# A transformer block with top-2 experts: inputs laid out transposed on the host, weight folds on TensorE, and another split of the batches over two groups

## The reference, cut to what matters

```python
Wm = W_attn + (lora_A @ lora_B).reshape(W_attn.shape)      # 384 x 128
xa = batchnorm(x @ Wm.T)            # mean and variance over all tokens
q, k, v = split(xa)
y = softmax(causal(q @ k.T / sqrt(128))) @ v
y = y @ W_proj.T @ (W_proj + lora_pA @ lora_pB).T
x = layernorm(x + y)
gates = top2(softmax((ln(x) * r_scale + r_bias) @ router_w.T + router_b))
h_e = gelu((ln(x) * scale_e + bias_e) @ w1[e].T + b1[e])    # 8 experts, 512 hidden
x = layernorm(x + sum_e gates_e * (h_e @ w2[e].T + b2[e]))
```

## Time and profile before

| what | us |
|---|---|
| median of three runs | 638.56 |
| the profiled execution, own time | 633.27 |
| its span, first to last instruction | 631.5 |
| start, until the first row maximum of the attention | 42.4 |
| attention, until the first tile's transpose | 185.5 |
| experts, 142 tiles | about 362 |
| tail after the last matmul | about 41 |

### The profile page before, as it was taken

One profiled execution on the slowest core, in us unless ns is written; L12 is line 12 of the kernel. 1 busy time (PEld: TensorE's weight loads), 2 busy tenths in 40 slices (PEclk: granted clock), 3 DMA queues, 4 the chain that ended last, 5 costly groups with the idle time before them and its releaser, 6 DMA issues.

```text
span 631.5 us, 15137 instructions
## 1 busy us (share of the span) xinstructions
PE 476.5 (75%) x3652; PEld 448.1 (71%) x3652; DVE 287.1 (45%) x1617; ACT 364.6 (58%) x934; POOL 301.9 (48%) x361
## 2 busy tenths in 40 slices
PE   7969566585756959777778887778899999999300
PEld 6868455575655859777767876777899999999300
DVE  0178454655545964222222221212333588783393
ACT  0338354553643866544454554445677788998483
POOL 4002655556552005445655444545344476675573
PEclk9979797897977979878889777788799999999755
DMA  9950111111112012222221221222122456543362
GB/s 227 358 147 14 44 44 40 35 40 44 39 44 62 2 32 69 59 60 78 74 66 56 57 56 54 58 61 60 53 65 80 139 155 168 168 121 115 91 195 72
DMA packets 66049, 53.70 MB, mean 85 GB/s; under 512 B 11986, under 2 KB 59218, under 8 KB 65970
## 3 DMA queue, kind: packets, MB, share of 16 engines
q1 hardware_dynamic: 53136, 33.27, 19.8%
q0 software_dynamic: 8640, 17.97, 8.7%
q10 hardware_dynamic: 4194, 1.53, 1.0%
HBM read 28.43 MB, written 24.31 MB: 84 GB/s over the span
## 4 chain that ended last, share of the span: by engine, by line
PE 64%; another core or an unknown queue 11%; issue 6%; ACT 6%; DVE 5%; DMA 5%; SPq 2%; ACTq 0%; POOL 0%; POOLq 0%; DVEq 0%
PE bank L803 24%; PE bank L813 22%; PE bank L796 3%; PE bank L705 3%; DMA ld_bc<-L_ffn_expert_ln_bias 2%; PE bank L691 2%; SPq L383 1%; PE bank L714 1%; PE bank L763 1%; PE bank L752 1%; DMA xT<-ybuf 1%; DMA x_all<-L_attn_x 1%; PE bank L765 1%; PE bank L764 1%
## 5 line engine op out<-in xcount | busy, mean ns | idle before, releaser
L549 POOL DMA_INDIRECT ybuf<-xT,yrow x142 | 137.3, 967 | 183.5 <-DVE yrow L1278 134.9
L803 PE MATMUL bank<-xT 128*128 128x128 f32 x1136 | 167.9, 296 | 34.3 <-issue 20.0
L803 PEld LDWEIGHTS bank<-xT 128*128 128x128 f32 x1136 | 152.3, 209 | 36.8 <-issue 21.6
L813 PE MATMUL bank<-w2T,xT 128*128 x1136 | 164.9, 292 | 13.1 <-ACT xT L948 11.5
L538 POOL DMA_INDIRECT queue<-x_all,pos_i x128 | 123.1, 962 | 94.6 <-DVE pos_i L1196 56.3
L813 PEld LDWEIGHTS bank<-w2T,xT 128*128 128x128 f32 x1136 | 150.7, 206 | 17.2 <-issue 16.7
L1268 DVE TENSOR_TENSOR xT<-bank,b_bc 128x128 f32<-128x128 f32 x142 | 41.4, 292 | 221.5 <-PE bank L813 120.4
L835 ACT ACTIVATE xT<-w1T,zero_col 128x512 f32 x142 | 102.3, 721 | 31.2 <-issue 24.0
L948 ACT ACTIVATE xT<-bank 128x512 f32<-128x512 f32 x142 | 82.7, 583 | 23.8 <-PE bank L803 21.0
L835 ACT ACTIVATE xT<-bank,one_col 128x128 f32<-128x128 f32 x142 | 51.6, 364 | 76.0 <-remote 35.7
L1275 DVE TENSOR_SCALAR xT<-xT 128x128 f32<-128x128 f32 x142 | 49.4, 348 | 2.4 <-issue 1.5
(11 more groups left out here) (220 smaller groups left out, 750.5 us busy)
## 6 DMA issues: line engine op xcount, KB each, us to landing
xT<-queue SPq DMA_DIRECT2D x142, 66.0 KB
xT<-ybuf SPq DMA_DIRECT2D x32, 256.0 KB
x_all<-L_attn_x SPq DMA_DIRECT2D x16, 256.0 KB, 6.2
w_rows<-L_ffn_w SPq DMA_DIRECT2D x16, 256.0 KB, 8.8
out<-x_all SPq DMA_DIRECT2D x32, 128.0 KB
ybuf<-xT,yrow POOLq DMA_INDIRECT x142
queue<-x_all,pos_i POOLq DMA_INDIRECT x128
queue<-pad_rows SPq DMA_DIRECT2D x2, 528.0 KB, 13.7
```

The lines of the kernel that those rows point to most:

```text
L549: pool.indirect_dma_start(out=ybuf, out_offset=bass.IndirectOffsetOnAxis(yrow[:, q:q + 1], 0), in_=ysb[:, q, :], in_offset=None).then_inc( ...
L803: last = mm(bank[2 + s][:, h * P:(h + 1) * P], w1c[:, (q - 1) % XR, h * P:(h + 1) * P], xgT[:, s, :], start=True, stop=True)
L813: last = mm(bank[4 + s][:, 0:P], hs[:, s, h, :], w2T[:, bass.ds(e, 1), h, :].rearrange("p a d -> p (a d)"), start=(h == 0), stop=(h == HC ...
```

## The change

The host now hands over x also transposed (`x_t`), w1 and w2 transposed, the small parameters packed in two arrays (`wide`, `low`) and b1 in three copies. Device code changes as follows.

- x chunks are loaded by SP (even) and ACT (odd); xT comes straight from `x_t` in eight loads of four batches. No transposes of x or of weights are left, nor their copies of x and w2.
- Two `fold_round`s in place of four. PE does seven matmuls on zeros before the first chunk.
- The scale, bias and b1 go into w1 on PE: per expert one float32 matmul with `fold_l[e]` (identity times scale, plus bias less scale over C) and one bfloat16 matmul that adds b1 in three parts. Three experts before the attention, five in steps 0 to 4, each with one copy by ACT. DVE's `fold_expert` is gone; it makes `dl`, `pick_b` and `b1s` in the start, ACT makes `fold_l`.
- DVE's second and third part of `split_constant` come after the row maxima of step 0; PE's `start_v(0)` waits for them (s_cv).
- NB0 is 18, so NTILE0 is 79 and group 1 has 63 tiles; COUNT0 is 21. BETWEEN is 5: 14 batches, before tiles 0, 5, ..., 65. LAG is 12, YR is 24; `yb` lies in the buffer of w1's rows. FIN stays at 18, so no batch is loaded ahead of `results_written(NTILE)`.
- In the tail a store is that of the batch five back.

```diff
-    NB0 = 20
+    NB0 = 18
-        XR, YR = 4, 16
+        XR, YR = 4, 24
-        LAG = 7
+        LAG = 12
-            BETWEEN = 6
+            BETWEEN = 5
@@ sync
-            for c in range(NCH):
+            def load_columns(c):
+                here = slice(c * XT_B * T, (c + 1) * XT_B * T)
+                sp.dma_start(xT[:, here], x_t[:, here]).then_inc(s_xt[c], 16)
+            for c in range(0, NCH, 2):
                 load_chunk(c)
+            load_columns(0)
             for e in range(E):
-                load_w1(e)
+                sp.dma_start(w1r[:, e], w1_t[:, e]).then_inc(s_w1[e], 16)
+                if e == E - 2:
+                    load_columns(1)
+            for c in range(2, NB // XT_B):
+                load_columns(c)
...
             for n in range(max(FIN, NB0), NB):
                 load_y(n)
-                store(stored)
-                stored += 1
+                if stored <= n - 5:
+                    store(stored)
+                    stored += 1
@@ tensor
+            def fold_w1(e):
+                pe.wait_ge(s_w1[e], 16)
+                if e == 0:
+                    pe.wait_ge(s_fl, 1)
+                    pe.wait_ge(s_b1s, 1)
+                wait(pe, s_wc, e if e > W1_FIRST else e - W1_FIRST + 1)
+                mm(fold_bank(e)[:], fold_l[:, e, :], w1r[:, e], start=True, stop=False)
+                mm(fold_bank(e)[:], pick_b[:, e, :], b1s[:], start=False, stop=True).then_inc(s_wt, 1)
...
-                if X_STEP <= k < W_STEP:
-                    transpose_chunk(EARLY_X + k - X_STEP)
-                elif W_STEP <= k < W_STEP + 2 * E:
-                    transpose_weights(k - W_STEP)
+                if k + W1_FIRST < E:
+                    fold_w1(k + W1_FIRST)
@@ scalar
+            act.dma_start(low_s[:], low).then_inc(s_small, 16)
+            act.dma_start(wide_s[:], wide).then_inc(s_small, 16)
+            act.dma_start(rb[:], r_b.unsqueeze(0)).then_inc(s_small, 16)
...
+            for c in range(1, NCH, 2):
+                act.dma_start(x_all[:, c * CH:(c + 1) * CH, DATA:DATA + P], x_chunks[c]).then_inc(s_x[c], 16)
+                if c == 3:
+                    act.dma_start(b1f[:], b1_rows).then_inc(s_b1f, 16)
...
+            for e in range(E):
+                last = act.activation(fold_l[:, e, :], ident[:], ACT.Identity, bias=dl[:, e:e + 1],
+                                      scale=lsT[:, e:e + 1])
@@ vector
-            v.wait_ge(s_ls, 48)
-            op(v.tensor_tensor(ld_bc[:], ld_bc[:], ls_bc[:], ALU.subtract))
-            op(v.tensor_scalar(b1c[:], b1c[:], 1.0 / C, None, ALU.mult))
...
-                if 0 <= k - FOLD_STEP < 3 * (E - 1):
-                    fold_expert(1 + (k - FOLD_STEP) // 3, (k - FOLD_STEP) % 3)
+                if known == 0:
+                    for n in range(1, 3):
+                        split_constant(n)
+                    v.sem_inc(s_cv, 1)
```

More of the change, by code:

```diff
@@ L222, in build, with fold_bank @@
         r_bias = sb("r_bias", [P, E])
[L225 to L247, removed]
+        w1r = sb("w1r", [P, E, H])
+        dl = sb("dl", [P, E])
+        fold_l = sb("fold_l", [P, E, P])
+        b1f = sb("b1f", [P, H])
+        b1p = sb("b1p", [P, H], BF16)
+        b1s = sb("b1s", [P, H], BF16)
+        own = sb("own", [P, E])
+        warm = sb("warm", [P, P])
+        pick_b = sb("pick_b", [P, E, P], BF16)
+        W1_FIRST = 3
+        def fold_bank(e):
+            return bank[(6, 4, 5)[e] if e < W1_FIRST else 6]
         s_w1 = [sem(f"s_w1_{e}") for e in range(E)]
-        s_w2, s_ls, s_w1p, s_wt, s_wc = [sem(n) for n in ("s_w2", "s_ls", "s_w1p", "s_wt", "s_wc")]
+        s_w2, s_wt, s_wc, s_dl, s_fl, s_b1s = [sem(n) for n in ("s_w2", "s_wt", "s_wc", "s_dl", "s_fl", "s_b1s")]
         U = 4
@@ L594, in _ @@
             mm, tr = pe.matmul, pe.transpose
-            pe.wait_ge(s_one, 1)
             gram = bank[7][:, 0:P + 1]
+            pe.wait_ge(s_warm, 1)
+            for n in range(N_WARM):
+                mm(bank[6][:, 0:P], warm[:], warm[:], start=True, stop=True)
             def fold_round(r):
@@ L654, in _ @@
             last.then_inc(s_gram, 1)
-            for c in range(2):
-                transpose_chunk(c)
             pe.wait_ge(s_cov, 1)
-            mm(bank[2][:, 3 * P + 2 * E:3 * P + 3 * E], wp2[:], wvvT[:, 0:E], start=True, stop=True)
             for g in range(3):
@@ L663, in _ @@
             last.then_inc(s_proj, 1)
-            for c in range(2, 9):
-                transpose_chunk(c)
+            mm(bank[2][:, 3 * P + 2 * E:3 * P + 3 * E], wp2[:], wvvT[:, 0:E], start=True, stop=True).then_inc(s_wr, 1)
+            for e in range(W1_FIRST):
+                fold_w1(e)
             pe.wait_ge(s_qk, 1)
@@ L868, in _, with copy_w1 @@
+            last.then_inc(s_fl, 1)
+            def copy_w1(e):
+                act.wait_ge(s_wt, e + 1)
+                cp(w1T[:, e, :], fold_bank(e)[:], bias=zero_col[:]).then_inc(s_wc, 1)
+            for e in range(W1_FIRST):
+                copy_w1(e)
             act.wait_ge(s_mt, 1)
@@ L1097, in _, with split_constant @@
             pg.settle()
-            for n in range(3):
+            def split_constant(n):
                 op(v.tensor_copy(cvp[:, n, :], cv[:]))
```

242 lines of the change are left out of this document (110 added, 132 removed).

## The result

The changed kernel takes **654.94 us** in the median of four runs (648.42 to 657.68), the kernel before beside it 638.72 (638.44 to 640.36): ratio 1.0258, 95% interval 1.0205 to 1.0310. It is slower by 16 us; 8 us faster was forecast, and 654.94 lies outside the range of 613 to 643. The profiled execution took 657.68 us (span 655.9, granted clock 0.836 against 0.873), 24.4 more than the 633.27 of before.

What follows compares the result with a forecast made beforehand. It took late PE signals at scatter bursts (stops), with no engine full in the attention, as the bound. Terms -7.0 + 2.2 - 26.3 + 5.6 + 14.6 + 3.1 gave -7.8 us: 630.7 us from 638.56, range 613 to 643.

Steps and rivals of the forecast that it cites:

- the stops: Attention and experts: PE's signal reaches ACT late at each scatter burst, costing 4.6 us in attention, 7.3 among tiles.
- Steps beside scatters: Attention: 17 steps for 19, each relieved by 0.7 us to 6.47, so -26.3 us, bounds -14.4 and -50.6.
- The first rival: Attention: stops set the pace, removed weight work is worth nothing; +4.1 us in all, 642.7 us; chance 0.22.
- The start: Up to the first row maximum: bias wait gone, 5.5 us, and 1.5 us gained at the Gram stage; -7.0 us.
- the Gram stage: Start, products of x with itself: 1.5 us gained despite 1.5 MB more loaded, bounds 3 gained and 1 lost.
- the cover: Start: three folds on PE lie beside DVE's statistics, some 3.4 us long; without that they cost 3.3 us.
- the third rival: Start: x's last chunk lands 5 us later, the start gains only 2, 635.7 us; chance 0.08 together with others.
- the sentence on rates: Start's loads: 244 GB/s with x's 512-byte rows, 335 with longer; added bytes take 4.6 us, or 6.1 by the rule.
- Steps 0 to 4: First attention steps: a fold of 1.1 us on PE in each, 18.0 us for 15.8, +2.2, bounds 0 and +5.
- Experts and tail: Tiles: two more bursts at 7.3 us, +14.6; end of kernel: 13 steps of 1.85 us for 11, +3.1.
- Buffers and lag: Experts: LAG 12 and YR 24 costed at nothing; without PE as cover they could gain 2 us.
- The second rival: Attention: POOL becomes the limit, 5.8 us a step, 619.2 us in all; chance 0.20.

Runs made afterwards that it cites:

- Without stops: Groups of runs on chips where no stop shows; the kernel before took 486.9, 488.3 and 488.2 us there, against 632.0 and 634.0 in the other groups.
- fifth group: Runs on one chip: the changed kernel with all x on SP's queue, new split kept, took 638.47 us against 633.99 for the kernel before, ratio 1.0061.
- both parts undone: Changed kernel with all x first on SP's queue and NB0 20, BETWEEN 6 as before: 629.59 us (ratio 0.9989) on one chip, 480.85 (0.985) on another.
- third and second group: Two sets of runs on different chips; the kernel before took 632.0 us in the third and 488.3 in the second.
- the one queue: Changed kernel with all 16 chunks of x on SP's queue, new split kept: ratio 1.0061 (638.47 us) on one chip, 1.0176 (493.25 us) on another.
- the spread: Changed kernel with x on SP's queue, NB0 20, BETWEEN 6, and the experts' scatters one to a tile: 620.0 us, ratio 0.9788; elsewhere 481.59 us, 0.9905.

## Why the prediction was wrong, point by point

**What bounds the kernel** was read rightly: the stops, beside the bursts. It was not asked what sets their pace, and the largest term of the sum hangs on that.

**Steps beside scatters: the step that failed most**, -8.2 us for -26.3. The term "I take 0.7 a step, because the engines wait on each other in a chain outside the stops" took all of the removed work as relief. The runs showed its lower end, nothing: 135.0 to 140.6 us without weight work and 136.3 with it for the same 80 scatters. The first rival was right that the removed work is worth nothing there, and it decided where the text said, at a relief under 0.24; its 642.7 us still fell short, by what the start lost. Part of it is that PE's work became slower as it became less: 4.57 us busy a step before, 4.38 to 4.73 without the weight work. Without stops there is a relief, 0.34. The text also counted by steps (17 for 19) where the bursts count: 18 batches for 20, which at 1.70 us a scatter are 122.4 us, -13.9. The 128.0 us of the changed kernel are 5.6 more than that; with x early and the same split the stage took 124.34 us in the fifth group. What the rest is made of stays open; executions of one kind differ by as much (135.0 to 140.6).

**The start**, +3.8 for -7.0. "I take 1.5 us gained, bounds 3 gained and 1 lost" for the Gram stage is the step. The bytes were summed as if x went first; the order of the issues on two queues was in the diff and not followed. The last matmuls of x came at 33.97 us, and the stage ended 9.8 us later than before, not 1.5 earlier. Behind it the 5.5 us of the bias wait did go: from the end of the Gram stage to the first row maximum it was 17.1 us before and is 11.1 now. It would have been 8.3, as with x early, had the folds been hidden and 1.1 us long; at the lower clock they held PE's next product back by 2.4 us. The text did name the cover, at a price of 3.3 us for the 2.4, and the third rival the mechanism, x late by 5 us for the 9.8. Undone alone it gives 16.1 us side by side without stops. With x early the first row maximum comes at 32.2 to 33.0 us, below the 34 to 36 of the text. Of the sentence on rates: 280 GB/s moved in the first 20 us and 386 in the next 20, with the DMA engines full in both, as before; what decided was which bytes went first.

**Steps 0 to 4**, +6.3 for +2.2. The text's terms (15.5 us of PE, five folds of 1.1, two chunks of 0.5 less) make 20.0, and the 18.0 that it took has no working; with the constant made early the stage does take 18.72. The rest is the first step, where PE stood 2.10 us for the constant, at 48.19, with the next batch's products queued behind it. That is 2.0 us, and in some executions the clock then costs 1.4 more: the same kernel took 20.73 us at a granted clock of 1.00 and 22.17 at 0.92 (both parts undone, third and second group), and the changed kernel 22.09 at 0.92. The text had that wait as 1.4 us "nothing in sum"; it showed behind the first row maximum and not ahead of it.

**Experts and tail** were right: +13.2 for +14.6 and +2.9 for +3.1; 13 stops, a price of 7.5 us each for 7.3, and 13 adds at 1.83 us for 1.85. **Buffers and lag** at nothing: right as far as the runs can tell. **The split** is +14.6 + 3.1 + 5.6 less two steps of 7.17 in the text's own terms, so +9.0; alone it measures some +15 us (+7.3 between profiled spans of two groups, 638.8 and 631.5), and more than 9 is not explained. So the change is slower for two reasons that have nothing to do with its main part, the new split and late x. Both undone together leave a ratio of 0.9989 in place of 1.0258, 17 us. What is left, the folded weights and the columns, is worth nothing that the runs with stops can tell, and 1.5% without stops.

The two do not add: some 15 and 12.5 us one by one, 17 together. Undoing the split on top of the one queue gives 1.0061 - 0.9989 = 0.0072, 4.6 us of median in two groups, and 12.0 between their profiled spans (636.6 and 624.6), of which the latter was the shortest of its ten runs; the intervals are 0.4% wide on each side. Where between 5 and 12 it lies was not settled.

**The second rival** (POOL the limit of the attention) is refuted with stops. Without them POOL is the limit, but of the transition to the experts: it is still scattering when the steps are done.

## What to carry to other kernels

Before work is taken out beside a wait, ask whether the wait's length depends on that work at all: here 0.7 us less work a step was worth nothing that could be measured. Look at the granted clock too, since an engine with less to do may be slower at it. When loads are dealt out to two queues, follow the issue times of the last critical one against whatever the other queue issues meanwhile; put the critical array whole ahead of the loads that can wait. And when a loop bound moves, look at what it sets elsewhere: a store that trails its load by two batches in place of four doubled a tail.

## What the runs showed that was not expected

- The same kernel takes 487 us on some chips and 632 to 639 on others, at equal instruction times (a scatter 0.96 us and 0.30 between, a plain tile 1.90 us on both). Between the profiled executions of the kernel before (631.5 and 484.4 us), some 145 of the 147 us lie in the attention beside the scatters and in the tiles, where ACT and DVE start late on what PE has finished, with waits marked "remote"; the faster one has no such wait. What makes a chip one or the other, no run tells.
- With stops, the pace follows the number of POOL's indirect transfers more closely than anything else in the stage: 136.3 / 80 = 1.70 us per transfer in the attention before, 135.0 / 80 = 1.69 to 140.6 / 80 = 1.76 without weight work, 128.04 / 72 = 1.78 after, and with the experts 17.0 / 9 = 1.89 for a cycle of five tiles. The late signal arrived 1.6 us after the run of transfers ended in both attention stops shown (95.1 and 96.72; 107.06 and 108.68). That a signal is held until POOL pauses was argued from this, and the spread's 2% fits it only loosely; it is not shown.
- ACT took 11.58 us for the issue of six chunks, 1.93 each; SP took 6.89 for eight, 0.86 each. It is not shown that ACT's queue is the slower one: the two engines issued other loads beside these, and SP's own issues of 256 KB took from 0.58 us each (seven of w1 in 4.08) to 1.47 each (eight of w2 in 11.72).
